# One subtraction of a macaron transformer block on VectorE, moved behind the next step's maxima

## The reference

```
x = x + 0.5 * ffn(LN(x))      # 256 -> 1024 (up, gate) -> 256, weights made ternary
x = x + attn(LN(x))           # 16 heads, 4 key/value heads, 128 features a head
x = x + 0.5 * ffn(LN(x))

attn: q, k, v = x @ Wq, x @ Wk, x @ Wv;  rotary embedding on q and k
      s = q k^T / sqrt(128), masked above the diagonal;  p = softmax(s)
      out = (p v) * head_scale, heads joined, @ Wo
```

## Time and profile before

| | us |
|---|---|
| median of 3 runs | 1088.46 (1087.54 to 1088.8) |
| the profiled execution's own time | 1088.83 |
| its span, first to last instruction | 1087.0 |
| PE busy | 1069.8 (98%) |
| DVE busy | 923.1 (85%) |
| ACT busy | 815.8 (75%) |
| POOL busy | 715.1 (66%) |

### The profile page before, as it was taken

How to read it: one execution, slowest core, us unless ns; L and a number is a source line. 1 busy time by engine, 2 the same in 40 slices (tenths; PEclk the granted TensorE clock), 3 DMA queues, 4 the chain that set the end, 5 groups by cost and what they waited for, 6 DMA issues and landing times.

```text
span 1087.0 us, 26892 instructions
## 1 busy us (share of the span) xinstructions
PE 1069.8 (98%) x8517; PEld 844.5 (78%) x8517; DVE 923.1 (85%) x2313; ACT 815.8 (75%) x2038; POOL 715.1 (66%) x906
## 2 busy tenths in 40 slices
PE   8999999999999999999999999999999999999998
PEld 5556566788888888888888888888888887566665
DVE  6787886899999999999999999999999997433333
ACT  6787997787888788887877878778787785444443
POOL 2566675777777777777777777777777774444443
PEclk9999999999999999999999999999999999999999
DMA  9522332234434343344333443334334343100101
GB/s 348 155 49 40 58 59 40 45 74 93 70 74 82 71 83 68 72 82 79 76 68 72 82 82 72 76 72 83 74 72 82 72 82 69 30 19 19 39 19 39
DMA packets 262166, 79.93 MB, mean 74 GB/s; under 512 B 249328, under 2 KB 260848, under 8 KB 261872
## 3 DMA queue, kind: packets, MB, share of 16 engines
q1 hardware_dynamic: 261696, 79.19, 35.1%
q10 hardware_dynamic: 432, 0.27, 0.1%
HBM read 12.85 MB, written 4.19 MB: 16 GB/s over the span
## 4 chain that ended last, share of the span: by engine, by line
PE 74%; issue 10%; POOL 6%; ACT 5%; DVE 4%; DMA 0%; POOLq 0%; DVEq 0%; ACTq 0%
PE bank L759 45%; PE bank L818 14%; POOL SCR L428 6%; PE bank L718 5%; PE bank L728 5%; PE bank L748 4%; ACT SCR L628 1%; DVE ARENA L1144 1%; ACT ARENA L635 1%; PE bank L677 1%; DVE SCR L962 1%; DVE bank L1168 1%; ACT SCR L502 0%; DVE X L952 0%; ACT SCR L517 0%
## 5 line engine op out<-in xcount | busy, mean ns | idle before, releaser
L453 POOL TENSOR_SCALAR SCR<-SCR,RI 128x128 f32<-128x128 f32 (+1 forms) x512 | 311.1, 608 | 44.2 <-DVE RI L1140 4.1
L628 ACT ACTIVATE SCR<-bank,NM 128x128 f32<-128x128 f32 (+1 forms) x512 | 208.5, 419 | 122.8 <-DVE NM L1168 122.7
L418 POOL TENSOR_TENSOR SCR<-SCR 128x512 f32<-128x512 f32 x160 | 203.4, 1271 | 146.0 <-DVE SCR L962 144.6
L428 POOL TENSOR_TENSOR SCR<-SCR 128x512 f16<-128x512 f32 x128 | 151.4, 1185 | 154.1 <-ACT SCR L517 152.0
L818 PE MATMUL bank<-SCR 128*128 128x128 f32 (+1 forms) x1024 | 193.7, 332 | 4.4 <-ACT SCR L628 3.3
L523 ACT COPY SCR<-bank 64x512 f32<-64x512 f32 x320 | 185.6, 580 | 14.2 <-PE bank L759 8.1
L981 DVE SCALAR_TENSOR_TENSOR SCR<-SCR,CS,bank 128x512 f32<-128x512 f32 x128 | 95.1, 743 | 115.9 <-PE bank L728 103.5
L1144 DVE TENSOR_TENSOR ARENA<-SCR,ARENA 128x768 f16<-128x768 f32 x128 | 186.7, 1459 | 4.8 <-ACT ARENA L635 3.9
L759 PE MATMUL bank<-WOH,ARENA 128*128 128x256 f16 x1024 | 188.3, 273 | 0.8 <-DVE X L1177 0.8
L1168 DVE CUSTOM_DVE_ANT_0 bank<-bank,MASK,SCQ 128x128 f32<-128x128 f32 (+1 forms) x512 | 182.8, 415 | 3.5 <-PE bank L818 2.7
L534 ACT ACTIVATE SCR<-bank,SU 128x512 f32<-128x512 f32 x128 | 87.7, 685 | 110.7 <-PE bank L718 110.5
(11 more groups left out here) (120 smaller groups left out, 1649.1 us busy)
## 6 DMA issues: line engine op xcount, KB each, us to landing
out<-X SPq DMA_DIRECT2D x7, 512.0 KB, 2.9
X<-in_x SPq DMA_DIRECT2D x1, 2560.0 KB, 11.2
ARENA<-in_wq SPq DMA_DIRECT2D x1, 2048.0 KB, 13.9
ARENA<-in_wo SPq DMA_DIRECT2D x1, 2048.0 KB, 18.8
SCR<-ARENA SPq DMA_TRANSPOSE x128, 3.6
X<-in_x SPq DMA_DIRECT2D x3, 512.0 KB, 9.9
X<-in_wu SPq DMA_DIRECT2D x2, 512.0 KB, 5.6
X<-in_wg SPq DMA_DIRECT2D x2, 512.0 KB, 7.4
```

The lines of the kernel that those rows point to most:

```text
L418: gp.tensor_tensor(dst, M1[:, m, :], M2[:, m, :], ALU.add).then_inc(add, 1)
L428: gp.tensor_tensor(HL[layer][:, f % 4, :], H32[layer][:, f % 2, :], HH[layer][:, f % 4, :], ALU.subtract).then_inc(s["hl_done"], 1)
L453: last = gp.tensor_scalar(EX[:, par, lo:hi], EX[:, par, lo:hi], RI[:, par, c:c + 1], PS, ALU.mult, ALU.mult)
L628: last = act.activation(EX[:, par, 384 * hh + lo:384 * hh + hi], SBK[hh][:, lo:hi], ACT.Exp, bias=NM[:, par, c:c + 1], scale=-1.0, accum_o ...
```

## The change

At index t DVE no longer computes the low half of the probabilities of step t - 3 at the end of the index, behind the reciprocal. It computes that of t - 4 in the first part of the index, right behind the maxima and before the rope of t. The subtraction and its wait and semaphore are now in a function `low`. Steps 0 and 1 keep their old place, as do 125 to 127 behind the last sample; step 124 takes the new place. All samples are concerned. Code of no other engine is changed.

```diff
                         maxima(t - 2, i % 2)
                     if early and i == 1:
                         maxima(0, 0)
+                    if real(b, i, 4) and not (isinstance(b, int) and (b == 0 and i < 6 or b == BATCH and i > 0)):
+                        low(t - 4, i % 2)
                     if real(b, i, 0) and not first:
                         rope_mul(r, m, PJ[m])
...
                         ve.reciprocal(RI[:, par, :], RS[:, par, :]).then_inc(rcp, 1)
-                    if real(b, i, 3):
-                        ve.wait_ge(p_hi, t - 2)
-                        par = (i - 3) % 2
-                        ve.tensor_tensor(PR[:, par, 768:1536], EX[:, par, :], PR[:, par, 0:768], ALU.subtract).then_inc(p_lo, 1)
+                    if isinstance(b, int) and (b, i) in ((0, 3), (0, 4), (BATCH, 0), (BATCH, 1), (BATCH, 2)):
+                        low(t - 3, (i - 3) % 2)
...
+            def low(e, par):
+
+                ve.wait_ge(p_hi, e + 1)
+                ve.tensor_tensor(PR[:, par, 768:1536], EX[:, par, :], PR[:, par, 0:768], ALU.subtract).then_inc(p_lo, 1)
```

## The result

The changed kernel takes 1163.04 us (median of 4 runs, 1162.57 to 1163.3) against 1088.43 us before: 1.0685 times as long, 95% interval 1.0673 to 1.0698. The forecast was 1151 us with a range of 1130 to 1178. Its profiled execution has a span of 1160.8 us.

The account below looks back on a forecast made before the run. PE was taken to set the pace, with DVE also full. Span 1087.0 + 62.3 (waits for later transposes) + 0.9 - 3.1 + 2.5 = 1149.6; medians lie 1.5 higher: 1151 us, range 1130 to 1178.

Parts of the forecast that it names:

- Port: DVE's low half would wait less for POOL in its new place: 1.0 us instead of 1.48, 0.48 us gained per step.
- T: Start of a step's maxima on DVE; forecast at best 0.93 us after the scores' start, 1.40 at i = 0 and 4.
- The turned probabilities: Values matmuls wait for the DMA transpose the low half releases, landing 3.84 us after it; PE waits 0.9 us.
- the sum: Step-by-step reckoning of one sample's eight score starts: 49.14 us instead of 44.99, +62.3 us over 15 samples.
- The scratch buffer: ACT's exponentials wait for the low half of two steps before, which reads the buffer they write; nearly always fits, no price.
- d: Time of the moved low half on DVE: taken as 1.0 us, with bounds 0.92 (POOL free) and 1.48 (as before).
- x: Start of a step's scores on PE, from which the forecast counts the other starts of the step.
- The ends: First sample's added wait +0.9 us, second and third samples' present waits absorbed -3.1, waits behind the last sample +2.5.
- Faster by DVE's relief: Rival: PE never waits for the transpose, so DVE's relief decides and early waits vanish; some 1080 us, chance 4%.
- Port kept busy: Rival: the low half waits behind all four POOL normalization instructions or stays at 1.48 us; 1184 us or more, 7%.
- Clock: Rival: PE's new waits bring its clock from 2.4 to 1.2 GHz; near 1220 us if a tenth is hit, 2%.

Follow-up runs that it names:

- e7: Kernel before the change, with POOL's rotation sum cut to 8 of 512 columns: 1076.36 us.
- e2: Changed kernel with four buffers for the exponentials, so they no longer wait for any low half; transpose unchanged: 1150.89 us.
- e1: Changed kernel, but the transpose is released by the high half and carries it twice, so values no longer depend on the low half: 1141.85 us.
- e3: Changed kernel with the transpose in two transfers, six blocks of the high half first, six of the low half behind the subtraction: 1146.48 us.
- e9: Changed kernel with the low half one place further back, behind the step's rope instead of before it: 1315.98 us.

## Why the prediction was right, and which terms were off

*Port.* Right. The low half took 0.961 us on average; I had taken 1.0 and given 0.92 and 1.48 as ends. Only some of the starts fell where I had put them: of 128, 60 at the end of a normalization instruction (most in its last 0.14 us), 31 at the end of a rotation sum, 36 with POOL idle. The medians of the three are 0.955, 0.956 and 0.955 us, so hardly anything of it was waiting. The port is worth at most 12 us in the old order (e7), and in the new one the relief pays for nothing, since T is tied to the scores.

*The turned probabilities.* Right, in place and size: e2, which keeps this tie alone, takes 49.02 us a sample against 49.14 in the sum, with each interval within 0.15 us, and 1150.89 us against 1151. The leg from low half to values was 3.75 us, not 3.84. In the changed kernel the five delays of the values add up to 4.3 us a sample against 4.5.

*The scratch buffer.* This is the step that was wrong, though the range held: "this wait nearly always just fits, with no price at d = 1.0". It costs 3.4 us a sample where the transposes do not wait (e1), and still 0.9 where they do (49.93 - 49.02). I had followed the exponentials only as far as the next scores. Behind them on ACT stand the high halves, the rows' high half and the swaps. The changed kernel at i = 2 to 4:

```profile
687.57 0.18 DVE L1142 RECIPROCAL RI<-RS 128x4 f32<-128x4 f32 x1
...
688.62 0.63 ACT L584 CAST NHL<-SCR 128x512 f16<-128x512 f32 x1
...
689.29 0.69 DVE L1202 TENSOR_TENSOR NHL<-SCR,NHL 128x512 f16<-128x512 f32 x1 [1.55 <-ACT NHL L584]
...
692.34 0.37 ACT L628 ACTIVATE SCR<-bank,NM 128x128 f32<-128x128 f32 x1 [1.88 <-DVE ARENA L1165]
...
695.70 1.48 PE L818 MATMUL bank<-SCR 128*128 128x128 f32 x8
695.78 2.37 ACT L523 COPY SCR<-bank 64x512 f32<-64x512 f32 x4
...
696.98 0.69 DVE L962 TENSOR_TENSOR SCR<-bank,COS 128x512 f32<-128x512 f32 x1 [0.99 <-ACT SCR L523]
...
698.19 0.35 DVE L1173 CUSTOM_DVE_ANT_0 bank<-bank,MASK,SCQ 128x128 f32<-128x128 f32 x1
```

DVE is ready for the row low half at 687.7 and must wait for ACT; the maxima of i = 3 come 2.0 us after their scores' start instead of 0.93; their exponentials leave ACT so late that it swaps the keys only at 695.78, behind the start of the scores (forecast: 1.03 before it). T at i = 4 is x + 2.49, not x + 1.4, the next scores wait for exponentials, and the interval takes 5.88 instead of 4.92 us. So the term that was off is T at i = 4, and behind it the interval from i = 4 to 5, at 0.96 us more than the sum gave it. The other seven intervals are together 0.17 us under the sum, so that a sample is 0.79 us over it, and 15 samples make the 12 us by which 1163 exceeds 1151. With four buffers (e2) this interval is 4.92 us again.

*The ends* (+0.9, -3.1, +2.5 us): together with the rest of the span they came out close. Fifteen samples make 74.4 us, against 73.8 between the spans, where I had given the ends 0.3. From the first scores to the last the trace grew by 74.1 us, ahead of them it lost 1.4 and behind them it gained 1.1; I did not separate the three terms further.

*The rivals.* Faster by DVE's relief: the relief is real and PE's waits came all the same. Port kept busy: no, 0.96 us. Clock: it stayed at 1.00 in the attention stage of the changed kernel, but the danger was nearer than the 2% that I gave it. In that stage e1, e2 and e3 show three, one and four stretches at 0.5, and e9 nineteen.

The range held the time because the tie that I priced hid most of the tie that I did not: each alone costs 3.4 to 4.1 us a sample, both together 5.0. That it held was in part luck: its width came from the port and from the DMA leg, not from this term. Where the priced tie was loosened the error came out in full: e3 was expected at 1095 to 1115 us and took 1146.48.

## What to carry to other kernels

A producer that is moved behind a later instruction has two kinds of dependents: who reads its result, and who waits to overwrite its input. Price both, each as if the other did not exist, and follow the second as far as everything that is queued behind the waiting instruction. Where two ties lie side by side, removing one shows the other's price and not its own; a control with both removed in the old and the new order is what tells them apart.

An engine at 99% of the stretch can still be off the path: what bounds a pipeline with two buffers may be how late its work stands, not how much it is. Here 0.35 us a sample came from moving 1.5 us of DVE's row work two or three steps later (with 0.6 us of ACT's), while a reordering that freed 3.2 us of DVE a sample lost 75 us.

## What the runs showed of the hardware

The low half, a DVE subtraction with both inputs in SBUF, took 0.96 us with POOL idle (median of 36 in the changed kernel; 0.92 in the earlier trace rows). Started 0.6 us into POOL's addition of 1.27 us it took 1.48 us and ended 0.81 us after that addition. Started in the last 0.14 us of one of POOL's four short multiplications it took 0.96 us still. In e2 some started earlier in such a multiplication, took up to 1.20 us, and also ended 0.80 us after it, though the next one stood behind it: the subtraction waits for the one instruction that is under way. The Trainium skill (SBUF — State Buffer, "Who interferes with whom") has such a subtraction contend with any POOL instruction that reads SBUF, the later one blocked for the whole of the earlier; the 1.48 and the 1.20 us agree.

A DMA transpose of 12 blocks landed 3.65 us after its issue in the changed kernel, one of 6 blocks 2.74 us in e3 (medians).

PE's clock fell from 2.4 to 1.2 GHz after a wait of 2.9 us in e9. In e1 and e3 it fell seven times in the attention stage, each time behind a single wait of 1.7 us, and it came back while PE was busy. One of the seven, in e1:

```profile
540.00:544.00 4.00, 2.27 (x18) 1.62 (x16) 3.81 (x12) 2.10 (x9) 1.86 (x2) 1.00 0.00 0
545.00:547.00 2.00, 2.00 (x14) 1.62 (x13) 1.86 (x6) 1.12 (x3) 1.85 (x3) 0.50 0.52 101
548.00:552.00 4.00, 4.00 (x38) 3.56 (x36) 2.08 (x9) 3.00 (x8) 2.98 (x5) 1.00 0.26 50
```

The same wait recurs in each sample of e1, and only three samples show the drop; what decides between them stays open. A drop made its sample 1.7 us longer in e1 (49.96 to 49.98 us instead of 48.31).
